# Last recurrence's elementwise chain at full width, with four smaller moves in the layers before it

## The reference

```python
x = x + _L0_cond_ref(...)   # gated wavelet up and down, gate from the condition
x = x + _L1_cond_ref(...)   # recurrence: h = tanh(x_t @ Wx + b + h @ Wh)
x = x + _L2_cond_ref(...)   # two shared experts; router picks 2 of 8 routed ones
x = x + _L3_cond_ref(...)   # leaky gated recurrence, below

def step(h, z_t):                                    # L3, 2048 steps in sequence
    gate = sigmoid(h @ Wh.T + z_t @ Wz.T + b)
    h_new = tanh(h * leak + gate * z_t)
    return (h_new, h_new)
```

## Time and profile before

| | |
|---|---|
| median of 3 runs | 2008.15 us (2004.0 to 2009.28) |
| profiled execution, own time | 2005.9 us |
| its span, first to last instruction | 2004.0 us |
| mean granted TensorE clock | 0.994 |
| first recurrence | 0 to about 270 us |
| shared part 0 | to 791 us |
| routed stage | to 1168 us |
| shared part 1 | to about 1700 us |
| last recurrence | to the end |

### The profile page before, as it was taken

The page is one execution under the profiler, slowest core; times in us unless marked ns, Lnnn a source line. Parts: engine busy times, 40 slices in busy tenths (PEclk is TensorE's granted clock), DMA queues, the critical chain, the costliest instruction groups (busy, mean ns, idle before and its releaser), DMA issues. The chain is left out here.

```text
span 2004.0 us, 45733 instructions
## 1 busy us (share of the span) xinstructions
PE 1954.9 (98%) x18204; PEld 1183.2 (59%) x18204; DVE 1104.4 (55%) x2342; ACT 800.6 (40%) x1685; POOL 143.8 (7%) x144
## 2 busy tenths in 40 slices
PE   8999979999999999999999999999999999999997
PEld 6999944444444443444444444444455555999996
DVE  5666556544896645111111147655665664778887
ACT  4444445432121433343333345322333332665554
POOL 0000000000000100121111111111110200000000
PEclk9999989999999999999999999999999999999999
DMA  7033247764342424999999866433332452001111
GB/s 297 20 136 140 106 140 221 197 169 137 122 173 84 168 89 147 234 205 204 202 207 201 187 199 193 127 90 96 107 92 60 114 167 89 24 3 43 42 42 45
DMA packets 281903, 266.38 MB, mean 133 GB/s; under 512 B 225991, under 2 KB 233293, under 8 KB 275086
## 3 DMA queue, kind: packets, MB, share of 16 engines
q1 hardware_dynamic: 270942, 228.73, 39.9%
q0 software_dynamic: 10800, 35.40, 6.6%
HBM read 153.70 MB, written 56.36 MB: 105 GB/s over the span
## 5 line engine op out<-in xcount | busy, mean ns | idle before, releaser
L1049 PE MATMUL sh_p<-xh,arena 128*128 128x512 f16 x2048 | 610.6, 380 | 8.9 <-DVE xl L1303 7.5
L1049 PE MATMUL sh_p<-xl,arena 128*128 128x512 f16 x1024 | 388.7, 380 | 0.0
L1049 PEld LDWEIGHTS sh_p<-xh,arena 128*128 128x128 f16 x2048 | 200.5, 98 | 251.8 <-issue 10.7
L1064 PE MATMUL p<-sh_h_hi,arena 128*128 128x512 f16 x1024 | 304.6, 379 | 0.0
L1804 DVE SCALAR_TENSOR_TENSOR ro_hs<-ro_h,fac,ro_hs 128x512 f16<-128x512 f32 x71 | 53.3, 751 | 303.9 <-ACT ro_hs L1790 259.6
L1218 ACT CAST sh_h_hi<-sh_half_h 128x512 f16<-128x512 f32 x128 | 79.1, 618 | 347.7 <-DVE sh_half_h L1569 347.7
L1747 PE MATMUL ro_pf<-arena,xres 128*128 x852 | 197.0, 381 | 8.3 <-PEq L883 4.3
L1212 ACT ACTIVATE sh_sig<-sh_p,fac 128x512 f32<-128x512 f32 x128 | 87.8, 686 | 290.5 <-PE sh_p L1049 290.5
L1747 PE MATMUL ro_py<-arena,ro_ht 128*128 x852 | 195.3, 379 | 0.7 <-DMA ro_ht<-ro_hs 0.7
L1064 PE MATMUL p<-sh_h_lo,arena 128*128 128x512 f16 x512 | 194.0, 379 | 0.0
L1566 DVE SCALAR_TENSOR_TENSOR sh_half_h<-sh_sig,sh_p 128x512 f32<-128x512 f32 x128 | 87.6, 684 | 153.2 <-ACT sh_sig L1212 153.1
(11 more groups left out here) (273 smaller groups left out, 3120.9 us busy)
## 6 DMA issues: line engine op xcount, KB each, us to landing
stage<-in_shared_w SPq DMA_DIRECT2D x29, 768.0 KB, 5.1
routed_rows<-xres SPq DMA_DIRECT2D x71, 256.0 KB
stage<-in_norms_r SPq DMA_DIRECT2D x16, 1024.0 KB, 4.8
stage<-in_routed_w SPq DMA_DIRECT2D x16, 1024.0 KB, 4.8
stage<-in_norms SPq DMA_DIRECT2D x14, 1024.0 KB, 5.0
arena<-x SPq DMA_DIRECT2D x12, 1024.0 KB, 6.2
rnn_xs<-in_x SPq DMA_DIRECT2D x8, 1024.0 KB, 19.1
x<-xres SPq DMA_DIRECT2D x16, 512.0 KB, 2.6
```

Source lines behind the costliest of these rows:

```text
L1049: mm = nc.tensor.matmul(p1[u % P1][:], arena[:, w:w + P], x[slot(gl)][:, :, k, :], start=(j == 0), stop=(j == 3 * KD - 1))
L1064: mm = nc.tensor.matmul(p2[m][:], arena[:, w:w + P], h[n % 2][:], start=(i == 0 and j == 0), stop=(i == HID - 1 and j == 2))
```

## The change

Five edits.

1. The last recurrence is built with `parts` = 1: sigmoid, multiply, add, both tanh and the low state each are one instruction of 128x256 instead of two of 128x128, with one semaphore step, and TensorE makes all 16 products of a kind before the next kind.
2. In the last recurrence VectorE makes x's low part before the output sum, not behind it.
3. The router's high and low weights lie side by side, so that one matmul by 16 columns takes the place of two by 8; VectorE adds the two halves with two operations.
4. The routed weights' cast and low part are made in two halves each, ordered by a new semaphore, and those that overwrite shared weights one item earlier (their loads too).
5. The two transposes of gathered rows are issued in item 58 instead of behind item 63.

```diff
@@ scan_layer, VectorE chunk
+                        if leaky and ahead is not None:
+                            low(q + 2, p, ahead, j)
                         if o is not None:
...
-                        if ahead is not None:
+                        if not leaky and ahead is not None:
                             low(q + 2, p, ahead, j)
@@ shared_part
-            return E_AT + j if last is None else (PART_GROUPS - 1) * HID + (last - 1) + 2
+            return E_AT + j if last is None else (PART_GROUPS - 1) * HID + (last - 1) + 1
...
+                        if n == ITEMS - 6:
+                            sp.wait_ge(stored[0], 16 * (PART_GROUPS // 2))
+                            for t in range(2):
+                                sp.wait_ge(keep["rows_in"][t], 16)
+                                sp.dma_start_transpose(turned_x(keep)[t].rearrange("p (q n) -> p q n", n=P), row_ring(keep, t)).then_inc(keep["xt_in"][t], 16)
...
                 if first_part:
-                    sp.wait_ge(stored[0], 16 * (PART_GROUPS // 2))
...
@@ TensorE logits
-                            for x, w in ((la_hi, wr_hi), (la_hi, wr_lo), (la_lo, wr_hi)):
-                                mm = nc.tensor.matmul(px[:, t * EXPERTS:(t + 1) * EXPERTS], x[:, k, t * P:(t + 1) * P], w[:, k, :],
+                            for x, w in ((la_hi, 2 * EXPERTS), (la_lo, EXPERTS)):
+                                mm = nc.tensor.matmul(px[:, 2 * t * EXPERTS:2 * t * EXPERTS + w], x[:, k, t * P:(t + 1) * P], wr_both[:, k, 0:w],
@@ ScalarE split_matrix
-                    nc.scalar.activation(arena[:, w0:w0 + MATRIX], stage[q % 2][:], ACT.Copy, scale=scl[:, col:col + 1]).then_inc(stage_hi, 1)
+                    for a in range(0, MATRIX, MATRIX // 2):
+                        b = a + MATRIX // 2
+                        nc.scalar.activation(arena[:, w0 + a:w0 + b], stage[q % 2][:, a:b], ACT.Copy, scale=scl[:, col:col + 1]).then_inc(matrix_hi, 1)
@@ VectorE split_matrix
-                    dve.wait_ge(stage_hi, LOADED + j + 1 - part_lead)
...
+                    for half in range(2):
+                        a, b = half * MATRIX // 2, (half + 1) * MATRIX // 2
+                        dve.wait_ge(matrix_hi, 2 * j + half + 1)
+                        lo = nc.vector.scalar_tensor_tensor(arena[:, w0 + MATRIX + a:w0 + MATRIX + b], stage[q % 2][:, a:b], scl[:, col:col + 1], arena[:, w0 + a:w0 + b],
+                                                            ALU.mult, ALU.subtract)
+                    lo.then_inc(stage_done, 1)
@@ VectorE scores
+                    nc.vector.scalar_tensor_tensor(part, both_halves[:, :, 0, :], fac[:, 5:6], keep["lt"][:].unsqueeze(1).broadcast_to([P, GROUP_TILES, EXPERTS]), ALU.mult, ALU.add).then_inc(logits_hi, 1)
+                    dve.wait_ge(logits_hi, a + 1)
+                    nc.vector.scalar_tensor_tensor(part, both_halves[:, :, 1, :], fac[:, 5:6], part, ALU.mult, ALU.add).then_inc(logits_out, 1)
@@ build
-        scan_layer(nc, "leaky", {}, x3, out, cond, ident, ones, 28, 0, True, 2, None, keep["scan"])
+        scan_layer(nc, "leaky", {}, x3, out, cond, ident, ones, 28, 0, True, 1, None, keep["scan"])
```

More of the change, by code:

```diff
@@ L810, in shared_part @@
             assert at[0] <= EBASE + 4 * KD * CW + 2 * KD * GW + 2 * GROUP_TILES * D
-            lead_hi, lead_done = sem("lead_hi"), sem("lead_done")
+            lead_hi, lead_done, matrix_hi = sem("lead_hi"), sem("lead_done"), sem("matrix_hi")
             la_in, la_hi_ready, la_lo_ready, row_turned, xt_stored, wr_hi_ready, wr_ready, logits_out = (
                 sem(n) for n in ("la_in", "la_hi_ready", "la_lo_ready", "row_turned", "xt_stored", "wr_hi_ready", "wr_ready", "logits_out"))
-            wrx, wr_hi, wr_lo = keep["wrx"], keep["wr_hi"], keep["wr_lo"]
+            wrx, wr_both = keep["wrx"], keep["wr_both"]
+            wr_hi, wr_lo = wr_both[:, :, 0:EXPERTS], wr_both[:, :, EXPERTS:2 * EXPERTS]
+            logits_hi = sem("logits_hi")
             const_in, zeroed, list_ready, list_used, listed = sem("const_in"), sem("zeroed"), sem("list_ready"), sem("list_used"), sem("listed")
@@ L1019, in _ @@
                 if first_part:
-                    sp.wait_ge(stored[0], 16 * (PART_GROUPS // 2))
-                    for t in range(2):
-                        sp.wait_ge(keep["rows_in"][t], 16)
-                        sp.dma_start_transpose(turned_x(keep)[t].rearrange("p (q n) -> p q n", n=P), row_ring(keep, t)).then_inc(keep["xt_in"][t], 16)
                     sp.wait_ge(xt_stored, 16 * LOOKS)
@@ L1074, in logits @@
                     for t in range(GROUP_TILES):
-                        i = 0
                         for k in range(KD):
-                            for x, w in ((la_hi, wr_hi), (la_hi, wr_lo), (la_lo, wr_hi)):
-                                mm = nc.tensor.matmul(px[:, t * EXPERTS:(t + 1) * EXPERTS], x[:, k, t * P:(t + 1) * P], w[:, k, :],
-                                                      start=(i == 0), stop=(i == 3 * KD - 1))
-                                i += 1
+                            for x, w in ((la_hi, 2 * EXPERTS), (la_lo, EXPERTS)):
+                                mm = nc.tensor.matmul(px[:, 2 * t * EXPERTS:2 * t * EXPERTS + w], x[:, k, t * P:(t + 1) * P], wr_both[:, k, 0:w],
+                                                      start=(k == 0 and x is la_hi), stop=(k == KD - 1 and x is la_lo))
                     mm.then_inc(px_filled, 1)
@@ L1204, in _ @@
                     split_tile(1)
-                    nc.scalar.activation(wr_hi[:], wrx[:], ACT.Copy, scale=scl[:, 3:4]).then_inc(wr_hi_ready, 1)
+                    nc.scalar.activation(wr_hi, wrx[:], ACT.Copy, scale=scl[:, 3:4]).then_inc(wr_hi_ready, 1)
                 else:
@@ L1428, in scores @@
                     dve.wait_ge(px_filled, a + 1)
-                    nc.vector.scalar_tensor_tensor(s[:, GROUP_TILES * a:GROUP_TILES * (a + 1), :], px[:, 0:GROUP_TILES * EXPERTS].rearrange("p (t e) -> p t e", e=EXPERTS),
-                                                   fac[:, 5:6], keep["lt"][:].unsqueeze(1).broadcast_to([P, GROUP_TILES, EXPERTS]), ALU.mult, ALU.add).then_inc(logits_out, 1)
+                    part = s[:, GROUP_TILES * a:GROUP_TILES * (a + 1), :]
+                    both_halves = px[:, 0:2 * GROUP_TILES * EXPERTS].rearrange("p (t h e) -> p t h e", h=2, e=EXPERTS)
+                    nc.vector.scalar_tensor_tensor(part, both_halves[:, :, 0, :], fac[:, 5:6], keep["lt"][:].unsqueeze(1).broadcast_to([P, GROUP_TILES, EXPERTS]),
+                                                   ALU.mult, ALU.add).then_inc(logits_hi, 1)
+                    dve.wait_ge(logits_hi, a + 1)
+                    nc.vector.scalar_tensor_tensor(part, both_halves[:, :, 1, :], fac[:, 5:6], part, ALU.mult, ALU.add).then_inc(logits_out, 1)
                 def weigh(number, a, kind, j):
@@ L1557, in _ @@
                     dve.wait_ge(wr_hi_ready, 1)
-                    nc.vector.scalar_tensor_tensor(wr_lo[:], wrx[:], scl[:, 3:4], wr_hi[:], ALU.mult, ALU.subtract).then_inc(wr_ready, 1)
+                    nc.vector.scalar_tensor_tensor(wr_lo, wrx[:], scl[:, 3:4], wr_hi, ALU.mult, ALU.subtract).then_inc(wr_ready, 1)
                 else:
@@ L1829, in build @@
                 "xres": [xres0, sm("xres1", [P, 2, KD, CW])], "xh": pair("xh", F16), "xl": pair("xl", F16),
-                "wr_hi": sm("router_hi", [P, KD, EXPERTS], F16), "wr_lo": sm("router_lo", [P, KD, EXPERTS], F16), "gsel": sm("gsel", [P, 2, TILES]), "slots": sm("slots", [P, 2, TILES], I32),
+                "wr_both": sm("router_both", [P, KD, 2 * EXPERTS], F16), "gsel": sm("gsel", [P, 2, TILES]), "slots": sm("slots", [P, 2, TILES], I32),
                 "token_of": sm("token_of", [P, SLOT_TILES], I32), "owner": sm("owner", [1, SLOT_TILES], I32),
```

2 lines of the change are left out of this document (removed).

## The result

The changed kernel takes 2046.36 us (median of 4 runs, 2042.85 to 2049.13), the kernel before 2008.03 (4 runs, 2004.0 to 2009.28): a ratio of 1.0188, with 95% between 1.0169 and 1.0207. Slower, as forecast, but by 38.3 us where 25 were forecast, and 5 us over the top of the range. The profiled execution has a span of 2045.8 us, 41.8 more than before, at a mean granted clock of 0.991.

What follows compares the result with a forecast made beforehand. TensorE, 98% busy, was taken as the bound, with the last recurrence's loop only 0.08 us shorter than its work per step. Terms +32.3 - 3.2 - 2.0 - 0.8 = +26.3 led to 2033 us, range 2024 to 2041.

Steps and rivals of the forecast that it cites:

- The mechanism: Last recurrence: at full width TensorE waits for the whole chain, idle about 0.45 us in each step.
- x's low part has no worth at full width: Last recurrence: making x's low part before the output sum wins 0, since TensorE has 0.45 us of slack per step.
- the low part of h is not late: Last recurrence: h's low part is ready before TensorE needs it; rival of a late one: 2047 us, 5%.
- The sign named for a failure: Last recurrence: a period over 3.6 us, meaning a second wait, would show the forecast wrong.
- The main term: Last recurrence: full-width chain makes the period 3.53 us, 91 periods 321.2 instead of 289.2, +32.0 us.
- The failed step: Last recurrence: all 91 periods reckoned at one period of 3.53 us, 321.2 us in total.
- the bounds given: Last recurrence: period between 3.48 and 3.58 us, making 27.7 to 36.8 us in all.
- The clock rival: Last recurrence: a bubble in every step lowers TensorE's clock; a tenth of steps hit gives +25, 2058 us; chance 3%.
- Boundary and logits: Block boundary before the routed stage comes earlier, -2.0 us; router with fewer, wider logit matmuls, -3.2 us.
- The split's move: End of first shared part: halved, earlier weight splits move the boundary from 790.8 to 788.8, -2.0 us.
- The routed stage: Shorter boundary gap of 2.3 us should keep TensorE's clock, 1.7 us back, half of it taken: -0.8 us.
- The other half of the term: Routed stage: TensorE waits longer for the next tile's transpose, which meets two loads; so only half of 1.7 us counted.

Runs made afterwards that it cites:

- The halves with one common wait: Changed kernel with the chain back in halves, TensorE waiting for both halves of the high state before its first state matmul: 2037.50 us, ratio 1.0149.
- The width alone: Kernel before with only the last recurrence's chain set to full-width instructions: 2050.36 us, ratio 1.0216.
- the splits back: Changed kernel with the chain in halves and the routed weights split as whole matrices, one item later again: 2001.25 us, ratio 0.9956.
- the filled end: Changed kernel with 12 extra input matmuls, results unused, in each of the last four steps: 2044.84 us, ratio 1.0183.
- Halves with the other edits: Changed kernel with the last recurrence's chain set back to halves, the other four edits kept: 1998.64 us, ratio 0.9953.
- the low part first, unrolled: Changed kernel with the chain in halves, x's low part also ahead of h's decay, and the 12 looped chunks written out: 1993.52 us, ratio 0.9924.

## Why the prediction was too low

**The mechanism held.** The chain of sigmoid, multiply, add and tanh sets every step; x's low part has no worth at full width; the low part of h is not late (no second wait in a step). The halves with one common wait show that TensorE's start on the first half is most of what is lost. The sign named for a failure, a period over 3.6 from a second wait, came with 3.67 and without that wait: the sign did not foresee a longer hand-over.

**The main term was mis-sized: +32.0 forecast, +43.5 measured.** The failed step reads "91 periods ... At 3.53 they are 321.2": one period for all steps. It came from rows that all had constant addresses and TensorE at full clock. The 11.5 us over it are:

- 0.03 in every step, 0.01 from the sigmoid to TensorE and 0.02 from there to the next sigmoid: 91 x 0.03 = 2.7. Inside the bounds given (3.58).
- The address instruction in the looped chunks: 5.4, shown by writing them out. The term was left out, and is over the bounds: 3.67 is more than the 3.58 at the top.
- 0.06 at each of the real chunks' starts (3.62 against 3.56), looped or not: 0.8.
- The clock at half in the last three periods: 0.36 + 1.11 + 1.11 = 2.6, shown by filling the idle time.

**The clock rival was right in kind and placed wrongly.** It was priced as steps lost anywhere in the recurrence, 25 us for a tenth of them, at 3%, and argued away with the last steps of the kernel before, where TensorE is 45% busy at 1.00. But there TensorE's weight load idled 1.46 us, and here it idles 2.1; the row was not the case that it stood for. The page of the Trainium skill named there, TensorE: Matmul & The Clock Gate, section "What's actually happening", has the clock follow how busy TensorE was recently, and in these three steps the trace agrees with it. The width alone, with the same steps at 1.00, shows that such idle time does not always bring the fall.

**Boundary and logits: right.** -4.65 against -5.2 together. The split's move was priced at 2.0 and comes to 1.7 by landmarks (from the first shared to the first routed matmul 514.9 us with the splits back and 513.2 with them in halves), by the medians 2.6; the transposes nothing. What is left is the logits': 518.0 before and 514.9 with the splits back, 3.1 of the 3.2 forecast, as 16 columns cost what 8 do.

**The routed stage: -0.8 forecast, +2.4 measured.** "The new gap is 2.3, so I expect the 1.7 back" failed in this profile: 6.95, 0.1 less than before. Then the fourth tile's 12 matmuls took 4.21 us instead of 2.76, +1.45, since the clock fell there too, and the two waits on the tiles' transposes came to 5.1 us instead of 4.0. Together that is the +2.4. The same reckoning holds in all 13 profiles: the stage takes between 369.6 and 370.0 us, plus TensorE's waits in it, plus half of the time that it stood at 0.50.

The forecast took it that the clock falls at the boundary or not at all, and rested on the fourth tile of the kernel before, which kept its clock after a wait of 3.33 us. That it was kept was chance: with the splits back it was lost there after 3.31. Seven of the nine kernels here with a gap of 2.3 to 2.4 us at the boundary did keep the clock there (24 matmuls in 5.35), two did not (the changed one and the filled end), and the gaps of 3.9 to 4.3 all lost it. But each of those seven lost it once at the third or fourth tile instead, for 3.4 us, as long as the kernel before did at the boundary. Halves with the other edits:

```profile
788.06 5.35 PE L1760 MATMUL ro_pf<-arena,xres 128*128 x24 [2.34 <-PEq L887]
804.51 4.45 PE L1760 MATMUL ro_pf<-arena,xres 128*128 x12 [2.60 <-DMA xres<-xl]
```

The other half of the term, that TensorE would wait longer for the transposes when it comes early, was right in kind: the seven wait 2.8 to 3.2 us at the third tile, the kernel before 0.7. What decides where the clock falls stays open.

**+1.0 in the second shared part** was not forecast; 0.7 of it is a wait on `sh_half_h` that stands in the waits above and not in the kernel with halves and the rest. It does not come with the change as such: the filled end, the same program up to its last four steps, has 536.7 us and no such wait, and the low part first, unrolled, has 537.7 with a wait of 0.9. Why it comes and goes is open.

The single profiles differ from the medians by up to 3 us. The kernel before's was 2.1 under its median (2005.9 against 2008.03), the changed one's 1.2 over (2047.57 against 2046.36), which is nearly all of the step from 38.3 to 41.8. The kernel before's profile stood at 0.50 for 3.4 us of its routed stage; the three others with a gap of 3.9 us or more at the boundary stood so for some 8.4 and took 379.1 to 379.3 us for it. Against those three the changed kernel's 378.8 is 0.4 less, so the +2.4 comes from that one low profile more than from the change.

## What to carry to other kernels

Where a chain of small operations closes a loop, its portions are worth what the neighbouring engines do between the first and the last of them: here 0.40 us of a step for TensorE's early start and 0.14 for the sigmoid's, against 0.05 that the shorter instructions cost in the chain. Price such a loop from a row of every kind of step (looped code with computed addresses, a chunk's start, the last steps without filler) and not from the clearest one: an address instruction that stands behind the wait costs 0.02 us while another engine sets the pace and 0.11 as soon as the chain does. A new idle time in every step also has to be compared by its length with an idle time at which the trace shows the clock kept.

## What the runs showed of the hardware

- TensorE's clock fell in the last steps at idle times of 1.9 to 2.0 us in two kernels, and not in a third with the same steps and a fourth with the same idle times. After a gap of 2.3 to 2.4 us at the block boundary it was kept in seven kernels and lost in two; after a wait of 3.3 us at the fourth routed tile it was kept in one (3.33) and lost in another (3.31).
- Matmuls by 16 columns start 0.025 us apart like those by 8, while those by 64 start 0.03 apart.
